# A Perceiver block on one core: the output weights of cross-attention are split earlier, in a place of their own, and each output projection moves one place ahead

## What is computed

```python
x = x + xattn(layernorm(x), ctx, mask, ...)   # 8 heads of 64; q and k with a LayerNorm per head; 257 context rows
x = x + attn(layernorm(x), ...)               # q, k, v: sigmoid(4 * (BatchNorm(x @ W) - 1)); weights from mean(q), mean(k)
x = x + ffn(layernorm(x), gate_w, w1, w2, w3) # 8 experts, the best 2 of each token, silu(x w1) * (x w3) @ w2
```

## Time and profile before

| what | value |
|---|---|
| median of 3 runs | 750.67 us (750.59 to 751.85) |
| profiled execution | 751.07 us, of it span 749.3 us |
| TensorE matmuls, share of the span | 96% |
| VectorE | 66% |
| ScalarE | 59% |
| GpSimd | 32% |
| mean granted clock of TensorE | 0.99 of full |

### The profile page before, as it was taken

How to read it: one execution, slowest core, us unless ns; L and a number is a source line. 1 busy time by engine, 2 the same in 40 slices (tenths; PEclk the granted TensorE clock), 3 DMA queues, 4 the chain that set the end, 5 groups by cost and what they waited for, 6 DMA issues and landing times.

```text
span 749.3 us, 14137 instructions
## 1 busy us (share of the span) xinstructions
PE 717.5 (96%) x4901; PEld 595.9 (80%) x4901; DVE 491.2 (66%) x902; ACT 442.2 (59%) x958; POOL 240.6 (32%) x209
## 2 busy tenths in 40 slices
PE   4899999999999999999999989999999979999996
PEld 3677888888888888888888877888778857888874
DVE  6766766675757667757567566967467866655573
ACT  4655675675657666756666566564655335555650
POOL 1462212121212112212122125753840023555525
PEclk9999999999999999999999999999999979999999
DMA  9941121212121212121212206531115457666648
GB/s 294 111 127 43 43 86 43 85 46 79 46 80 42 84 42 84 42 84 42 84 42 85 100 2 181 170 120 51 57 42 196 139 169 242 109 107 106 107 77 327
DMA packets 59672, 75.21 MB, mean 100 GB/s; under 512 B 8784, under 2 KB 33360, under 8 KB 59632
## 3 DMA queue, kind: packets, MB, share of 16 engines
q1 hardware_dynamic: 52032, 58.16, 26.2%
q0 software_dynamic: 4720, 11.27, 8.3%
q10 hardware_dynamic: 2880, 5.24, 1.9%
HBM read 54.75 MB, written 19.92 MB: 100 GB/s over the span
## 4 chain that ended last, share of the span: by engine, by line
PE 86%; DVE 5%; DMA 3%; ACT 2%; issue 2%; POOL 1%; SPq 0%; POOLq 0%; DVEq 0%
PE pK L32 42%; PE pV L32 11%; PE pP L32 9%; PE pV L1625 5%; PE pT L1526 4%; PE pT L1714 4%; PE pS L1669 2%; PE pP L1696 2%; PE pT L1861 2%; DMA fin<-total 1%; PE pT L1506 1%; PE pS L1791 1%; DMA total<-big,idx 1%; PE pS L1884 1%; DVE bst L995 1%
## 5 line engine op out<-in xcount | busy, mean ns | idle before, releaser
L32 PE MATMUL pK<-parts 128*128 128x512 f32 x840 | 211.3, 399 | 1.5 <-POOL parts L576 1.5
L535 POOL TENSOR_TENSOR parts<-big,parts 128x1024 fp32r<-128x1024 f32 x32 | 77.7, 2428 | 311.3 <-ACT parts L762 311.3
L32 PEld LDWEIGHTS pK<-parts 128*128 128x128 f32 x840 | 152.0, 188 | 32.2 <-POOL parts L576 2.0
L1037 DVE TENSOR_TENSOR kn<-pK,head_rs 128x512 f32<-128x512 f32 x62 | 42.9, 692 | 58.3 <-ACT head_rs L676 58.3
L32 PE MATMUL pK<-w,lhs 128*128 x276 | 69.2, 399 | 0.9 <-DVE sq L1442 0.3
L32 PEld LDWEIGHTS pK<-w,lhs 128*128 128x128 f32 x276 | 50.4, 189 | 12.1 <-issue 2.4
L32 PE MATMUL pP<-pT,parts 128*128 128x256 f32 x384 | 52.7, 287 | 0.0
L1452 DVE TENSOR_TENSOR w_p<-big,w_p 128x1024 fp32r<-128x1024 f32 x22 | 27.0, 1225 | 38.2 <-ACT w_p L952 38.2
L1031 DVE TENSOR_REDUCE head_ss<-sq 128x8 f32<-128x512 f32 x62 | 42.5, 685 | 13.1 <-ACT sq L670 13.1
L610 POOL DMA_INDIRECT big<-x_rows,idx_x x23 | 26.8, 1164 | 74.0 <-DVE idx_x L1408 59.5
L670 ACT ACTIVATE sq<-pK 128x512 f32<-128x512 f32 x62 | 36.9, 595 | 23.1 <-PE pK L32 23.1
(11 more groups left out here) (322 smaller groups left out, 1469.3 us busy)
## 6 DMA issues: line engine op xcount, KB each, us to landing
big<-in_ctx_dram SPq DMA_DIRECT2D x32, 512.0 KB, 3.8
total<-zero SPq DMA_DIRECT2D x32, 256.0 KB, 4.0
w_raw<-in_L_ffn_w_dram SPq DMA_DIRECT2D x16, 512.0 KB, 5.9
big<-in_L_ffn_w_dram SPq DMA_DIRECT2D x8, 512.0 KB, 4.8
fin<-total SPq DMA_DIRECT2D x8, 512.0 KB, 8.0
x_rows<-big ACTq DMA_DIRECT2D x8, 256.0 KB, 2.1
total<-big ACTq DMA_DIRECT2D x8, 256.0 KB, 2.3
big<-in_x_dram SPq DMA_DIRECT2D x1, 1536.0 KB, 10.2
```

Source lines behind the costliest of these rows:

```text
L32: last = pe.matmul(out, lhs(a, c), rhs(b, c), start=start and c == first and n == 0, stop=stop and c == chunks - 1 and n == 2)
L535: nc.gpsimd.tensor_tensor(ctxN[:, u, LO], ctx_raw[:, u], ctxN[:, u, HI].bitcast(F32), ALU.subtract).then_inc(cn_lo, 1)
L1037: tt(heads(kn[:, t]), heads(pKV[t][:, :]), per_head(head_rs[:, t]), ALU.mult).then_inc(k_n, 1)
```

## The change

The split of xo gets a place of its own, in the upper half of `w_p` (free once the first keys are made), and is made in the loop's surroundings: ScalarE's high parts behind batches 2 and 3, VectorE's low parts behind batches 3 and 28. Output tiles 0 and 1 get buffers of their own (`out_first`, in free halves of the key weights' rows) and are split behind batches 28 and 29 (ScalarE) and 30 and 31 (GpSimd). With it, projects 0 to 7 move: 0 into batch 31, 1 and 2 ahead of the transposes of batch 32, 3 behind them, 4 behind the batch, 5 to 7 behind the transposes of LayerNorm tiles 8 to 10. ScalarE's and VectorE's lists follow. On GpSimd the scaled weights of aq stand behind output tile 4 instead of 3, aq's low part behind tile 6 instead of 5. Since the low half of `xT` moves to 32 KB, the experts come in another order (`COMES`), 5 in the place of 2.

```diff
-        xo_p = parts[:, 4 * C * D:6 * C * D].rearrange("p (s c n) -> p s c n", s=2, c=C)
+        xo_p = w_p[:, 2 * C * D:4 * C * D].rearrange("p (s c n) -> p s c n", s=2, c=C)
+        out_first = [[at(f"out_first{t}{s}", [P, C, P], (18 + 4 * (2 * t + s)) * KB, F32R) for s in (HI, LO)] for t in range(2)]
-        xT = at("xT", [P, 2, C, TILES * P], 64 * KB, F32R)
+        xT = [at("xT_hi", [P, C, TILES * P], 64 * KB, F32R), at("xT_lo", [P, C, TILES * P], 32 * KB, F32R)]
...
+        COMES = (0, 1, 5, 3, 4, 2, 6, 7)
+        PLACE = {e: i for i, e in enumerate(COMES)}
+        out_of = lambda t, s: out_first[t][s][:, :, :] if t < 2 else out_p[:, t % 2, s]
...
@@ GpSimd
             for b in (B - 2, B - 1):
                 queries(b, b % 2)
                 ctx_parts(b, b % 2)
+                out_low(b - (B - 2))
...
-            low_part("xo", XO_ORDER[:1])
-            for t in range(TILES):
-                if t == C:
+            for t in range(2, TILES):
+                if t == C + 1:
                     for c in range(C):
                         bn_weight(0, c)
-                if t == C + 2:
+                if t == C + 3:
                     low_part("aq")
                 out_low(t)
@@ ScalarE, batch
                 if not main:
-                    out_high(2)
+                    ln_root(TILES)
...
                 if not main:
-                    out_high(3)
-                    ln_root(TILES)
+                    ln_root(TILES + 1)
+                    out_high(4)
                     bn_root(0)
...
                 if main and not nxt:
-                    high_part("xo", XO_ORDER)
                     act.wait_ge(pc_mm, (b - 1) * 2 + 2)
-                    out_high(0)
+                    out_high(2)
@@ ScalarE, behind the batches
             for r in range(1, BT):
                 batch(0, r, first=r == 1)
+                if r >= 2:
+                    high_part("xo", (2 * r - 4, 2 * r - 3))
...
             for r in range(BT):
                 batch(TILES - 1, r, nxt=r < BT - 1)
-            out_high(1)
+                if r < 2:
+                    out_high(r)
+            out_high(3)
             batch(TILES, 0, main=False, nxt=False)
-            out_high(4)
-            ln_root(TILES + 1)
             out_high(5)
+            out_high(6)
...
-                if t + 4 < TILES:
-                    if t + 5 == TILES:
-                        act.wait_ge(o_out, TILES)
-                    out_high(t + 4)
+                if t == 2:
+                    act.wait_ge(o_out, TILES)
+                    out_high(TILES - 1)
@@ VectorE, batch
+                if not main:
+                    out_add(0)
                 if nxt:
                     ctx_low(b + 1, 1 - u)
...
                 if not main:
-                    out_add(0)
+                    out_add(1)
...
                 if not main:
-                    out_add(1)
                     ln_norm(TILES, x_all[:, 0])
+                    out_add(2)
                     bn_scale(0)
...
-                if main and not nxt:
-                    for c in XO_ORDER[1:]:
-                        dve.wait_ge(w_hi, high_count("xo", c))
-                        tt(xo_p[:, LO, c], raw("xo")[:, c], xo_p[:, HI, c].bitcast(F32),
-                           ALU.subtract).then_inc(w_lo[JOB["xo"]], 1)
@@ VectorE, behind the batches
+            def output_weight_low(chunks):
+                for c in chunks:
+                    dve.wait_ge(w_hi, high_count("xo", c))
+                    tt(xo_p[:, LO, c], raw("xo")[:, c], xo_p[:, HI, c].bitcast(F32),
+                       ALU.subtract).then_inc(w_lo[JOB["xo"]], 1)
...
                 batch(0, r, first=r == 1)
+            output_weight_low((0, 1))
...
                 batch(TILES - 1, r, nxt=r < BT - 1)
+                if r == 0:
+                    output_weight_low((2, 3))
             batch(TILES, 0, main=False, nxt=False)
-            out_add(2)
             ln_norm(TILES + 1, x_all[:, 1])
+            out_add(3)
             bn_shift(0)
-            out_add(3)
             out_copy(TILES - 1)
@@ TensorE, batch
+                if main and not nxt:
+                    pe.wait_ge(k_n, b * MT + 1)
+                    project(0)
                 if not main:
-                    project(0)
                     project(1)
+                    project(2)
...
                 if not main:
-                    project(2)
+                    project(3)
@@ TensorE, behind the batches
-            project(3)
+            project(4)
             out_tile(TILES - 1)
             for t in range(TILES):
                 ln_turn(TILES + t)
-                if t + 4 < TILES:
-                    project(t + 4)
+                if t + 5 < TILES:
+                    project(t + 5)
                 elif t >= 5:
                     z_product(t - 5)
```

More of the change, by code:

```diff
@@ L258, in perceiver_block @@
         w_hi, w_centred, w_scaled = sem("w_hi"), sem("w_centred"), sem("w_scaled")
-        XO_ORDER = (3, 0, 1, 2)
         SPLIT = tuple(n for n in JOBS if n != "xv")
-        high_count = lambda name, c: SPLIT.index(name) * 4 + (XO_ORDER.index(c) if name == "xo" else c) + 1
+        high_count = lambda name, c: SPLIT.index(name) * 4 + c + 1
         w_sum = sem("w_sum")
@@ L417, in load_expert @@
             def load_expert(e):
-                if e >= 4:
-                    sp.wait_ge(w13_hi, e - 3)
+                i = PLACE[e]
+                if i >= 4:
+                    sp.wait_ge(w13_hi, i - 3)
                 for lo, w in ((0, w1), (F, w3)):
-                    sp.dma_start(w13_raw[e][:, :, lo:lo + F], chunked(w[e])).then_inc(w13_in[e % 4], 16)
+                    sp.dma_start(w13_raw[e][:, :, lo:lo + F], chunked(w[e])).then_inc(w13_in[i % 4], 16)
             sp.wait_ge(k_t, B * MT)
@@ L434, in _ @@
             sp.wait_ge(xo_mm, TILES)
-            load_expert(2)
+            load_expert(5)
             load_weight("av", "aq")
@@ L440, in _ @@
             sp.wait_ge(z_mm, 3 * TILES)
-            for e in (4, 5, 6):
+            for e in (4, 2, 6):
                 load_expert(e)
@@ L569, in _, with out_low @@
                     ctx_parts(b, u)
+            def out_low(t):
+                pool.wait_ge(oT_hi, t + 1)
+                nc.gpsimd.tensor_tensor(out_of(t, LO), qoT[:, :, t * P:(t + 1) * P],
+                                        out_of(t, HI).bitcast(F32), ALU.subtract).then_inc(oT_lo, 1)
             for b in (B - 2, B - 1):
@@ L890, in _ @@
                 if n in (4, 6, 8):
-                    w13_high(n // 2 - 2)
+                    w13_high(COMES[n // 2 - 2])
                 if TILES + 2 <= n < TILES + 6:
@@ L911, in _ @@
                 if 1 <= s <= 6:
-                    w13_high(4 + (s - 1) // 2, slice(2 * ((s - 1) % 2), 2 * ((s - 1) % 2) + 2))
+                    w13_high(COMES[4 + (s - 1) // 2], slice(2 * ((s - 1) % 2), 2 * ((s - 1) % 2) + 2))
                 if s - 2 >= 0:
@@ L1240, in w13_low @@
             def w13_low(e, part=slice(0, C)):
-                dve.wait_ge(w13_hi, e + 1 if e < 4 else 11 if e == 7 else 2 * e - 4 + part.start // 2 + 1)
+                i = PLACE[e]
+                dve.wait_ge(w13_hi, i + 1 if i < 4 else 11 if i == 7 else 2 * i - 4 + part.start // 2 + 1)
                 tt(w13[:, e, LO, part], w13_raw[e][:, part], w13[:, e, HI, part].bitcast(F32),
@@ L1282, in _ @@
                 if n in (6, 8, 10):
-                    w13_low(n // 2 - 3)
+                    w13_low(COMES[n // 2 - 3])
                 if n == 3 * TILES - 2:
@@ L1361, in _ @@
                     for c in (2 * (s % 2), 2 * (s % 2) + 1):
-                        w13_low(4 + (s - 2) // 2, slice(c, c + 1))
+                        w13_low(COMES[4 + (s - 2) // 2], slice(c, c + 1))
                 if s == TILES - 2:
```

18 lines of the change are left out of this document (7 added, 11 removed).

## The result

The changed kernel takes 746.36 us in the median of four runs (746.18 to 746.60), the kernel before 751.17 in the same comparison (750.59 to 751.85): a ratio of 0.9938 with a 95% interval of 0.9922 to 0.9954. It is faster by 4.8 us where 2.1 were forecast, and lies under the range.

What follows compares the result with a forecast made beforehand. TensorE's matmuls fill 96% of the span, so time is won only where it waits or runs slow; VectorE then caps the gain. -2.3 + 0.2 = -2.1 us from 750.67 gives 748.6, range 746.9 to 750.8.

Steps and rivals of the forecast that it cites:

- Project 0 in the hole: Batch 31, where TensorE ran dry at 444.64: project 0 fills it until 447.5; products at 449.6, scores at 452.6.
- The low clock: TensorE around 447 us: clock at 0.50 costs 1.66 us on key transposes and first products; disappears with the change.
- The third wait: After the last scores, TensorE waiting on GpSimd's low part of output tile 0: project 1 starts 1.6 us sooner.
- TensorE alone: If only TensorE counted, the self-attention products would start 1.6 + 2.9 = 4.5 us sooner.
- VectorE becomes the bound: VectorE's queue before z product 0: 3.15 us sooner less 0.9 waiting for ScalarE, so 2.3; TensorE waits about 1.5.
- GpSimd's order at 0: GpSimd's output tiles and aq weights reordered: tile 7's low part ends at 479.3, project 7 due 479.5; cost 0.
- The split in the loop, 0.2: Splits of xo after batches 2, 3 and 28: a stall of 0.2 us taken, in batch 4.
- Rival D: After batch 3, VectorE's second subtraction meets GpSimd's context subtraction, TensorE stalls 2.4 us: 751.0 or 752.6; chance 0.08.
- B: VectorE isn't the bound, GpSimd's overlaps fall away, TensorE keeps 4.5 - 0.2: 746.4; sign z product 0 before 484.5; chance 0.17.
- A: The forecast itself: VectorE's queue caps the gain at 1.6 to 2.8 us, less 0 to 0.4: 747.9 to 749.4; chance 0.50.
- C: The new wait before z product 0 lets the clock fall, costing 1.66 us: 750.2; chance 0.15.
- E: GpSimd's part of tile 7 or projects' waits on VectorE's adds come 2 us late: 750.3 to 750.7; chance 0.10.

Runs made afterwards that it cites:

- the early split without the collision: Against the kernel before: only the early splits of xo and output tiles 0 and 1, with GpSimd's tile 1 ahead of batch 31's context subtraction; 747.75 us beside 750.48, 0.9963.
- the run with ScalarE's wait taken away: Against the changed kernel: ScalarE's high part of output tile 7 behind the root and high part of LayerNorm tiles 11 and 9; 746.40 us, ratio 0.9940 to the kernel before.
- the piece behind it shortened: Against the changed kernel: ScalarE's high part of output tile 7 later, and VectorE's bn_scale(1) behind tile 11's low part; 749.15 us, ratio 0.9981 to the kernel before.
- the later ones: Two further comparisons of the unaltered changed kernel with the kernel before: 746.80 us beside 749.09 (0.9963), and 747.91 beside 749.89 (0.9973).
- the early split alone: Against the kernel before: only the early splits of xo and output tiles 0 and 1 in places of their own, projects unmoved; 749.14 us beside 749.09, 0.9991.
- the hole left open: Against the changed kernel: project 0 put back into batch 32, ahead of projects 1 and 2; 750.34 us beside 749.09 for the kernel before, ratio 1.0007.

## Why the prediction was right and wrong

*Project 0 in the hole: right, 0.3 us too late.* Products were due 8.56 us behind the scores of batch 30 and the next scores 11.56 (449.6 and 452.6 from 441.04); they came at 8.27 and 11.27.

*The low clock: right in the trace, wrong as a property of the kernel.* The clock is 1.00 throughout. But the 1.66 us counted in the ceiling was that of one trace: three others of the kernel before wait as long and keep it. It was worth 1.3 us in z product 0. The prediction's reading of a low slice in the middle of the earlier trace rows is wrong as well; only the earlier trace rows show this fall. The prediction had a rival for a fall behind the new wait, and none for a before without one.

*The third wait: right.* Project 1 follows the scores; the early split without the collision is 1.6 us faster by stage, as the step says.

*TensorE alone: right.* z product 0 is 3.48 us nearer and 1.28 was waited for ahead of it: 4.76 us where 4.5 stands.

*"VectorE becomes the bound": the step that failed, by its size.* The new wait is where it should be (tile 13's transposes on the low part of tile 11, 1.28 us for "about 1.5"), but z product 0 came 3.48 us nearer where the cap said 2.3. It is the sum "3.15 less 0.9" that was mis-sized: as the start of the norm of tile 11 it was right, and everything behind that start was carried over from before unchanged. The norm started at 476.08 instead of 479.02, 2.94 us sooner, or 2.35 when the 0.59 of the execution is taken off, for 2.25 by the sum. The lines of before that it was carried over from are these:

```profile
478.94 1.32 POOL L576 TENSOR_TENSOR parts<-qoT,parts 128x512 fp32r<-128x512 f32 x1
...
479.02 1.52 DVE L1005 TENSOR_SCALAR big<-big,mean_var,ln_rs 128x512 f32<-128x512 f32 x1
```

There the norm started 0.08 us behind GpSimd's low part of output tile 6 and ended 0.28 behind its end. In the new order it started 0.65 us ahead of the end of aq's low part, and took 0.93. That is 0.59. From its end to that of the low part of tile 11 it was 6.36 us instead of 6.89, of which 0.41 is the wait of the norm of tile 12 for its root, which is gone. 2.35 + 0.59 + 0.53 = 3.47. The 0.59 comes from GpSimd's queue, which the prediction puts at 0. By its own schedule aq's low part was done at 478.0, and a norm that ends 0.28 behind it ends at 478.3, just where the sum has it (476.8 + 1.52). It was done at 476.73, or 477.32 with the 0.59 us of the execution put back: the scaled weights started at 463.45 so counted, not at 464, and aq's low part took 5.27 instead of 5.74. The prediction had said that it couldn't place the overlaps and gave them 0.7 to both sides; the miss is 1.2.

Ahead of that norm VectorE's queue gained and lost about as much, which is why its start was right: the norm of tile 9 took 0.78 for 1.47, the first instruction of the shift 1.49 for 1.77 and the wait of 0.33 went, while 1.25 came in ahead of out_copy(7).

Nor is VectorE's queue the only bound. Up to the norm of tile 11 GpSimd's queue sets the time, as the run with ScalarE's wait taken away shows, and with the piece behind it shortened TensorE's wait stays at 1.07, the latency of tile 11's turn. The prediction has the first as a bound (1.6 if the norm also meets GpSimd) and the second in no rival.

*GpSimd's order at 0: right for project 7, which is what the step asks.* Tile 7's low part ends at 478.17 and project 7 starts at 478.36, 0.2 us later (forecast 479.3 and 479.5). Undone, the order costs 7.7 us. What the step lacks is that the same queue sets when the norm of tile 11 ends.

*The split in the loop, 0.2: right.* VectorE's context subtractions start at 103.85 (forecast 103.94), the 21 matmuls take 5.18 us for 5.05, and the scores of batch 4 come 0.14 us later. Rival D didn't come.

*The rivals.* By its own sign (z product 0 before 484.5) and by its time, 746.4, B came nearest: overlaps fell away, as it says. But TensorE did not keep all its 4.5 us; a wait on VectorE remained, as A says. C and E didn't come.

*The difference to the runs.* -4.8 us in the first comparison, -2.3 and -2.0 in the later ones, for -2.1. The forecast's ratio, 0.9972, lies in the two later intervals and outside the first. The 2.7 us between -4.8 and -2.1 are 1.2 of the mis-sized sum, 0.59 and 0.7 that this pair of executions differs by ahead of and behind the stage, and the 0.2 charged for the loop. The agreement of the later comparisons is in part luck and isn't the sum made good: its cap had the clock's recovery in it. By the same working on a trace that keeps the clock (1.3 us less) the forecast would have been a gain of 1.0 by stage, where 2.3 was measured. How much of the first comparison's extra 2.5 us is the clock in before's four runs stays open; only one of them was profiled.

## What to carry to other kernels

When an instruction of VectorE is held by one of GpSimd, its end hangs on GpSimd's end: a wait ahead of it costs nothing as long as the instruction still starts before GpSimd's ends, and taking the wait away gains nothing. So schedule both queues and compare ends, and don't carry a duration over from a trace in which the two met otherwise. Before a low clock is counted as something to win, look whether other executions of the same kernel have it; and when a cap is named, ask which chain lies right under it.

## What the runs showed of the hardware

**A two-number instruction waits for the rest of one of GpSimd.** p_scale (128x2, both inputs in SBUF) took 0.16 us alone and 0.97 to 1.04 when GpSimd's 1.3 us subtraction had started 0.29 to 0.35 us sooner. The Trainium skill (SBUF — State Buffer, "Who interferes with whom") says that a VectorE instruction with two inputs in SBUF contends with one of GpSimd that reads SBUF, that the shared port pair is locked exclusively, and that the order of issue decides who is blocked. The traces agree: p_scale ended 0.01 to 0.02 us behind GpSimd's subtraction in the two timelines shown, and its small size didn't help it.

**A held norm ends with GpSimd's instruction.** The norm of a LayerNorm tile (128x512, one input in SBUF beside the two numbers a row) took 0.53 to 0.55 us alone. That of tile 11 began beside an instruction of GpSimd in all 18 traces, took 0.66 to 1.69, and ended 0.28 to 0.29 us behind the end of that instruction, or of the one that followed it at once.

**The same waits don't decide the clock.** Waits of 1.48 and 0.57 us were followed by 0.50 (1.2 GHz) in one execution of before; 1.52 and 0.53 in another, and 1.48 and 0.57 again in two more, were not. 2.30 us was followed by 0.50 with the early split alone, and not with the hole left open, both on chip 3. 5.82 us was, with 1.4 us more for the twelve matmuls behind it.

**Single executions of one kernel differ by up to 2.8 us** behind z product 0, to the end of the span: the early split with tile 1 sooner took 260.9 us in one and 263.7 in another, on two chips. By stage this whole change is worth 2.3.
